# The value column that a transposing attention kernel multiplies apart: eight 32-column matmuls once in four steps, in place of four once in two

## The chip, the cores and the metric

The kernel runs on one core of one Trainium2 chip. The metric is device time in microseconds (us) of one execution. Five engines run their own instruction streams and meet at semaphores: TensorE (PE in the profile; PEld is its weight loads), VectorE (DVE), ScalarE (ACT), GpSimd (POOL) and SyncE (SP).

## The reference

Two layers, each cross-attention followed by a mixture of experts, on 1024 query rows of width 128 and a context of 6404 rows:

```python
x = x + tanh(g_xattn[0]) * L0_xattn(ctx, layernorm(x), mask, ...)   # keys: 6404 context rows and 1024 latents
x = x + tanh(g_ffn[0])   * L0_ffn(layernorm(x), ...)                # 8 experts, top 2
x = x + tanh(g_xattn[1]) * L1_xattn(layernorm(x), ctx, ...)         # keys: one null key and 6404 context rows
x = x + tanh(g_ffn[1])   * L1_ffn(layernorm(x), ...)
# both attentions: 16 heads of 64; softmax(q @ k.T) @ v, then an output projection
# L0 alone: q and k are each divided by the root mean square of their 64 elements (qn, kn)
```

The whole is float32. The kernel holds that precision by splitting operands into a high and a low part.

## The kernel before

The attention layer (`attention_layer`, called once with L = 0 and once with L = 1) works in 4 **groups** of 4 heads. Within a group, the keys are cut into tiles of 128; L0 has 59 tiles and L1 has 51. Four tiles are a **chunk**; L0 has 14 full chunks and L1 has 12, and 3 tiles are left as a tail. The loop is: group, chunk pair (a hardware loop), chunk of the pair (`half`), then `u` from 0 to 3, then the chunk's four tiles, taken two by two (`t` is 0, then 2). `u` picks a head pair (`u // 2`) and half of the queries (`u % 2`).

One **step** is one tile for one `u`: scores of 128 keys by 2 heads by 512 queries, an exponential, and the products with the values. One **unit** is the four steps of one `u`. There are 14 x 4 x 4 = 224 units in L0 and 12 x 4 x 4 = 192 in L1, beside a tail of 12 steps in each of the 8 groups. The two pairs of a unit are called the **first pair** (`t` is 0) and the **second pair** (`t` is 2) here.

TensorE's order in a pair is written out by hand:

1. `score` (L815), twice, for the two steps after this pair: 12 matmuls on 64 rows each (64*128 in the profile), two at a time beside each other, one on the upper and one on the lower half of the array. It waits until the exponentials of this pair's steps are done (`p_ready`).
2. `mix_last` (L823), twice: 4 matmuls with 32 weight columns (128*32). The output has 128 partitions: 64 high values of a head, 63 low values and the row of ones. The low part of the 64th value column has no room there; these matmuls compute it, in one bank (`spare_ps`, 32 partitions for each head and each parity of the step).
3. In the second pair only, `project_kv` (L796): 3 matmuls for keys and values of a tile of the next chunk. It writes the bank `proj_ps`, so it waits until VectorE has taken the low part of the keys out of that bank (`k_low`, L639).
4. `mix_high` (L833), twice: 4 matmuls of the probabilities' upper 16 bits, read as bfloat16, with the values. In the first pair each of the two halves of `out_ps` must have been added to `out_acc` by VectorE (`add_out`, L647).
5. `mix_low` (L840), twice: 4 matmuls of the probabilities' rest (`probs_lo`, made by VectorE in `p_lo`, L634).
6. In the first pair only, `transpose_k` (L802): two transposes of the projected key rows, which ScalarE then reads as `k_hi` (L547) and VectorE as `k_lo` (L639). In L0 GpSimd normalises these rows first (`k_norm`: a power, L485, then a product, L487), from a variance that VectorE computes (`k_var`, L619 and L621); in L1 it doesn't, and the transposes wait for ScalarE's copy alone.

VectorE's order in a unit is `p_lo` of the two steps of the second pair, `v_lo` (L627, L629), `k_low`, `p_lo` of the next unit's first two steps, `add_out` of the first half, `k_var`, `add_out` of the second half. ScalarE's is two exponentials (L553), then copies of keys or values. In the fourth unit of each chunk ScalarE also makes the high part of the next context chunk (L558) between two exponentials, and GpSimd its low part (`x_low`, L493).

A step's probabilities lie in buffer `n % NB` of `probs`. No engine waits for a buffer by name; the order of TensorE's work keeps a buffer from being written too early.

Of the kernel before, what the change touches and what calls it, by code (L numbers as in the profile page):

```python
# [40 lines left out]
GH = 4  # L41
NG = H // GH
CT = 4
NPAIR = GH // 2
NB = 4
NPL = 4
VW = 36
TAIL = 3
# [103 lines left out]
def attention_layer(nc, A, L, sem_, sb_, layer_norm, rstd, B):  # L152
# [7 lines left out]
    NFULL = (NTILES - TAIL) // CT  # L160
# [13 lines left out]
    with scope:  # L174
# [262 lines left out]
        def item_no(g, c, j):  # L437
            return g * NITEM + c * CT + j
# [4 lines left out]
        with nc.Block() as block:  # L443
# [343 lines left out]
            def _(pe):  # L787
# [31 lines left out]
                def mix_last(n_, u, t, par):  # L819
                    p, n = u // 2, u % 2  # L820
                    for e in range(2):
                        j = 32 * (2 * e + n_ % 2)
                        last = nc.tensor.matmul(last_ps[j:j + 32, :], vlast[:, par, 2 * p + e, t, 4 - 4 * n:36 - 4 * n],  # L823
                                                p_hi[:, n_ % NB, e * 512:(e + 1) * 512],
                                                start=False, stop=True, skip_group_check=True)
                    return last
# [30 lines left out]
                with pe.Fori(0, NG) as g:  # L857
                    def transpose_q(p):
                        for t in range(QT):
                            last = nc.tensor.transpose(scores[:, p, t * P:(t + 1) * P],  # L860
                                                       qf.rearrange("p (t a e) d -> p t a (e d)", a=NPAIR, e=2)[:, t, p, :],
                                                       ident[:, :])
                        last.then_inc(qt_done, 1)

                    pe.wait_ge(fin_read, ONE + g * QT)
                    project_kv(g, 0, 0)
                    transpose_k(g, 0, 0)
                    project_kv(g, 0, 1)
                    pe.wait_ge(q_final, g + 1)
                    transpose_q(0)  # L870
                    transpose_q(1)
                    transpose_k(g, 0, 1)
                    for j in range(2, CT):
                        project_kv(g, 0, j)
                        transpose_k(g, 0, j)
                    project_kv(g, 1, 0)
                    pe.wait_ge(q_lo_done, (g + 1) * NPAIR)
                    score(0, 0, 0, 0, item_no(g, 0, 0))
                    score(1, 0, 1, 0, item_no(g, 0, 1))
                    pe.wait_ge(e_read, ONE + g)  # L880
                    for j in range(4):
                        nc.tensor.matmul(last_ps[32 * j:32 * j + 32, :], zero32[:, :],
                                         vlast[:, 0, :, :, :].rearrange("p h t k -> p (h t k)")[:, 0:512],
                                         start=True, stop=True, skip_group_check=True)
                    with pe.Fori(0, PAIRS) as i:
                        for half in range(2):
                            c = i * 2 + half
                            for u in range(GH):
                                for t in range(0, CT, 2):
                                    n = (half * GH + u) * CT + t  # L890
                                    s = g * NSTEP + i * (2 * GH * CT) + n
                                    for k in range(2):
                                        n2 = n + 2 + k
                                        half2, u2, t2 = n2 // (GH * CT), n2 // CT % GH, n2 % CT
                                        item = g * NITEM + i * (2 * CT) + half2 * CT + t2 if u2 == 0 else None
                                        score(n2 % 2, u2, t2, half2 % 2, item, s + k)
                                    for k in range(2):
                                        if u == 0:
                                            pe.wait_ge(v_ready, item_no(g, c, t + k) + 1)
                                        pe.wait_ge(p_ready, s + k + 1)  # L900
                                        mix_last(n + k, u, t + k, half)
                                    if t == CT - 2:
                                        if u < GH - 1:
                                            project_kv(g, c + 1, u + 1)
                                        else:
                                            project_kv(g, c + 2, 0)
                                    for k in range(2):
                                        mix_high(n + k, u, t + k, half, g * NUNIT + c * GH + u)
                                    for k in range(2):
                                        mix_low(s + k, n + k, u, t + k, half, CT - 1)  # L910
                                    if t == 0:
                                        transpose_k(g, c + 1, u)
                    for n in range(0, GH * TAIL, 2):
                        s = g * NSTEP + NFULL * CT * GH + n
                        for k in range(2):
                            n2 = n + 2 + k
                            if n2 < GH * TAIL:
                                u2, t2 = n2 // TAIL, n2 % TAIL
                                if L == 1 and n2 == TAIL - 1:
                                    pe.wait_ge(null_fix, 3 + g + 1)  # L920
                                score(n2 % 2, u2, t2, 0, item_no(g, NFULL, t2) if u2 == 0 else None, s + k)
                        tiles = [(n + k, (n + k) // TAIL, (n + k) % TAIL) for k in range(2)]
                        for k, (n_, u, t) in enumerate(tiles):
                            if u == 0:
                                pe.wait_ge(v_ready, item_no(g, NFULL, t) + 1)
                            if L == 1 and n_ == TAIL - 1:
                                pe.wait_ge(null_in, (g + 1) * (16 * (2 + GH)))
                            pe.wait_ge(p_ready, s + k + 1)
                            last_e = mix_last(n_, u, t, 0)
                        same = tiles[0][1] == tiles[1][1]  # L930
                        for k, (n_, u, t) in enumerate(tiles):
                            mix_high(n_, u, t, 0, g * NUNIT + NFULL * GH + u)
                            if not same:
                                mix_low(s + k, n_, u, t, 0, TAIL - 1)
                        if same:
                            for k, (n_, u, t) in enumerate(tiles):
                                mix_low(s + k, n_, u, t, 0, TAIL - 1)
                    last_e.then_inc(e_done, 1)

                    project_q(g * (GH * DH) + GH * DH)  # L940

                    pe.wait_ge(o_added, (g + 1) * (2 * NUNIT) + 2 * ONE)
                    pe.wait_ge(e_read, ONE + g + 1)
                    pe.wait_ge(kn_ready if QK_NORM else kv_read, (g + 1) * NKV)
                    pe.wait_ge(we_in, (g + 1) * (16 * 4 * GH))
                    for t in range(QT):
                        if t >= 2:
                            pe.wait_ge(fin_read, ONE + g * QT + t - 1)
                        for h in range(GH):
                            at = (h // 2) * (D + 1)  # L950
                            e0 = DH * (h % 2)
                            nc.tensor.matmul(fin_bank(t, h % 2)[:, at:at + D + 1],
                                             oacc[:, h, t * P:(t + 1) * P],
                                             w_o[:, bass.ds(g * GH + h, 1), :].rearrange("p h n -> p (h n)"),
                                             start=h // 2 == 0, stop=False, skip_group_check=True)
                            last = nc.tensor.matmul(fin_bank(t, h % 2)[:, at:at + D],
                                                    esb[e0:e0 + DH, (t % 4) * P:(t % 4 + 1) * P], w_e[e0:e0 + DH, h, t // 4, :],
                                                    start=False, stop=True, skip_group_check=True)
                        last.then_inc(fin_mm, 1)
# [219 lines left out]
```

## Time and profile before

| | us |
|---|---|
| three runs | 4977.56, 4981.62 (median), 4983.63 |
| the profiled execution, its time | 4978.31 |
| its span, first to last instruction | 4976.5 |
| TensorE matmuls busy | 4373.9 (88%) |
| VectorE busy | 3684.0 (74%) |
| ScalarE busy | 2963.1 (60%) |
| GpSimd busy | 953.1 (19%) |

The span is the profiled execution from its first to its last instruction, and its own time is 1.8 us more. A matmul's end is modelled in the profile, so a matmul of 512 columns is listed with about 0.39 us while the next one starts about 0.23 us after it: lengths of stretches are taken from start to start. The main loops take 512 + 511 + 512 + 511 us in L0 and 428 + 427 + 428 + 428 us in L1, at a granted clock of 1.00 (2.4 GHz).

### The profile page before, as it was taken

What the parts mean: (1) busy time and instruction counts of PE and PEld (TensorE: products, weight loads), DVE (VectorE), ACT (ScalarE), POOL (GpSimd) and SP (SyncE); (2) the same over time, 40 slices, a digit from 0 to 9 for tenths busy, and PEclk for the clock granted to TensorE, in tenths of its full rate; (3) what the DMA queues carried; (4) which work ended last, traced back from release to release, by engine and by line L of the source; (5) the groups of instructions that cost most, each with busy time, mean ns of one, the idle gap of its engine ahead of it and who ended that gap; (6) DMA issues with size and microseconds to landing.
All of it is one profiled execution on the core that took longest, in us unless ns stands there. A gap on an engine that the chain in (4) does not pass through costs nothing. (4 is left out here: it accounts for less than half of the span.)

```text
span 4976.5 us, 75660 instructions
## 1 busy us (share of the span) xinstructions
PE 4373.9 (88%) x25271; PEld 2648.0 (53%) x25711; DVE 3684.0 (74%) x5350; ACT 2963.1 (60%) x4610; POOL 953.1 (19%) x687
## 2 busy tenths in 40 slices
PE   2899978999779998799989499979999799979996
PEld 1455544555545555455556355545555455545554
DVE  5788867888668886688861577757776677767775
ACT  2677736777457774677732377736774577647761
POOL 2333323333233332333310100000000000000000
PEclk7999988999889999899999699989999899989997
DMA  1000000000000000000000100000000000000000
GB/s 49 1 0 0 0 3 1 0 0 0 3 1 0 0 0 1 0 0 0 0 34 1 47 0 0 0 3 0 0 0 3 1 0 0 2 0 0 0 0 9
DMA packets 15438, 19.58 MB, mean 4 GB/s; under 512 B 2704, under 2 KB 11256, under 8 KB 15096
## 3 DMA queue, kind: packets, MB, share of 16 engines
q1 hardware_dynamic: 9204, 14.52, 1.0%
q10 hardware_dynamic: 6148, 3.89, 0.3%
q8 instruction: 57, 0.93, 0.1%
q14 instruction: 29, 0.24, 0.0%
HBM read 17.87 MB, written 0.52 MB: 4 GB/s over the span
## 5 line engine op out<-in xcount | busy, mean ns | idle before, releaser
L634 DVE TENSOR_TENSOR a_probs_lo<-a_probs 128x1024 fp32r<-128x1024 f32 x1760 | 2193.3, 1282 | 650.8 <-ACT a_probs L553 650.4
L553 ACT ACTIVATE a_probs<-scores_ps,a_c_neg 128x1024 f32<-128x1024 f32 x1760 | 1876.5, 1111 | 878.3 <-PE scores_ps L815 878.3
L840 PE MATMUL out_ps<-a_probs_lo,a_v 128*128 128x512 f32 x3520 | 1142.1, 445 | 0.0
L833 PE MATMUL out_ps<-a_probs,a_v 128*128 128x512 bf16 x3080 | 846.9, 388 | 87.9 <-issue 64.0
L815 PE MATMUL scores_ps<-a_q_hi,a_k_hi 64*128 64x512 f32 x3520 | 792.8, 445 | 6.7 <-DVE a_k_lo L751 5.9
L840 PEld LDWEIGHTS out_ps<-a_probs_lo,a_v 128*128 128x128 f32 x3520 | 660.9, 188 | 224.3
L815 PE MATMUL scores_ps<-a_q_lo,a_k_hi 64*128 64x512 f32 x3520 | 705.7, 393 | 0.0
L815 PE MATMUL scores_ps<-a_q_hi,a_k_lo 64*128 64x512 f32 x3520 | 700.7, 392 | 0.0
L647 DVE TENSOR_TENSOR a_out_acc<-out_ps,a_out_acc 128x512 f32<-128x512 f32 x896 | 598.5, 689 | 99.8 <-PE out_ps L840 91.3
L493 POOL TENSOR_TENSOR a_chunk_lo<-a_keys_in_T,a_chunk_hi 128x512 fp32r<-128x512 f32 x120 | 229.8, 1915 | 1792.4 <-ACT a_chunk_hi L558 1792.4
L485 POOL TENSOR_TENSOR a_k_stat<-a_k_stat,minus_half 128x4 f32<-128x4 f32 x244 | 247.6, 1015 | 1482.0 <-DVE a_k_stat L621 1482.0
L833 PEld LDWEIGHTS out_ps<-a_probs,a_v 128*128 128x128 f16 x3520 | 268.6, 96 | 471.3 <-issue 171.2
L815 PEld LDWEIGHTS scores_ps<-a_q_hi,a_k_hi 64*128 64x128 f32 x3520 | 333.5, 185 | 289.0 <-issue 251.9
L796 PE MATMUL proj_ps<-a_w_kv_hi,a_chunk_hi 128*128 128x512 f32 x456 | 238.2, 522 | 204.9 <-DVE a_k_lo L639 128.9
L547 ACT ACTIVATE a_k_hi<-proj_ps 128x256 fp32r<-128x256 f32 x448 | 172.5, 385 | 375.8 <-PE proj_ps L802 375.7
L487 POOL TENSOR_TENSOR normed<-normed,a_k_stat 128x256 f32<-128x256 f32 x244 | 373.4, 1530 | 19.1
L815 PEld LDWEIGHTS scores_ps<-a_q_lo,a_k_hi 64*128 64x128 f32 x3520 | 336.2, 185 | 74.5
L823 PE MATMUL spare_ps<-a_probs,a_v_last 128*32 128x512 bf16 x3520 | 360.2, 399 | 0.0
L526 ACT ACTIVATE normed<-proj_ps 128x256 f32<-128x256 f32 x456 | 174.0, 382 | 310.3 <-PE proj_ps L796 310.3
L815 PEld LDWEIGHTS scores_ps<-a_q_hi,a_k_lo 64*128 64x128 f32 x3520 | 336.2, 187 | 37.7
L543 ACT ACTIVATE a_v<-a_v 128x512 fp32r<-128x512 f16 x448 | 290.5, 648 | 0.1
L802 PE MATMUL proj_ps<-identity,normed 128*128 128x128 f32 x896 | 191.9, 297 | 99.5 <-POOL normed L487 89.0
(189 smaller groups left out, 3606.5 us busy)
## 6 DMA issues: line engine op xcount, KB each, us to landing
squares<-in_L_xattn_Wkv SPq DMA_DIRECT2D x16, 128.0 KB, 2.4
m_w<-in_L_ffn_w1T SPq DMA_DIRECT2D x1, 2048.0 KB, 7.7
m_w<-in_L_ffn_w2T SPq DMA_DIRECT2D x1, 2048.0 KB, 12.1
a_w_q<-in_L_xattn_Wq ACTq DMA_DIRECT2D x2, 512.0 KB
a_w_e<-in_L_xattn_Wout SPq DMA_DIRECT2D x64, 0.5 KB
a_w_e<-in_L_xattn_Wo SPq DMA_DIRECT2D x64, 0.5 KB
residual<-in_x SPq DMA_DIRECT2D x1, 512.0 KB, 3.9
a_w_o<-in_L_xattn_Wout ACTq DMA_DIRECT2D x1, 512.0 KB
```

What stands on the lines that cost most here:

```text
L485: nc.gpsimd.tensor_tensor(kst[:, 2, :], kst[:, 1, :], mhalf[:, 0:GH], ALU.pow).then_inc(kn_rstd, 1)
L487: nc.gpsimd.tensor_tensor(krow, krow, over(kst[:, 2, :], [P, GH, DH]), ALU.mult).then_inc(kn_ready, 1)
L493: nc.gpsimd.tensor_tensor(x_l[:, :], x, x_h[:, :].bitcast(F32), ALU.subtract).then_inc(x_lo, 1)
L543: nc.scalar.activation(v32[:, par, :, j, :], v16[:, par, :, j, :], ACT.Copy).then_inc(v_ready, 1)
L553: nc.scalar.activation(probs[:, n % NB, :], scores[:, n % 2, :], ACT.Exp, bias=cneg[:, p:p + 1]).then_inc(p_ready, 1)
L634: nc.vector.tensor_tensor(plow[:, n % NPL, :], probs[:, n % NB, :], p_hi[:, n % NB], ALU.subtract).then_inc(plo_ready, 1)
L647: nc.vector.tensor_tensor(oacc[:, 2 * p + e, q], outs[:, e * 512:(e + 1) * 512], oacc[:, 2 * p + e, q], ALU.add).then_inc(o_added, 1)
L796: last = nc.tensor.matmul(proj[:, :], x[:, j * P:(j + 1) * P], w[:, :], start=n == 0, stop=n == 2)
L815: last = nc.tensor.matmul(scores[:, b, e * 512:(e + 1) * 512], kk[r, par, p, t, :], qq[r, p, n * 512:(n + 1) * 512], start=m == 0, stop=m ...
L823: last = nc.tensor.matmul(last_ps[j:j + 32, :], vlast[:, par, 2 * p + e, t, 4 - 4 * n:36 - 4 * n], p_hi[:, n_ % NB, e * 512:(e + 1) * 512] ...
L833: nc.tensor.matmul(outs[:, e * 512:(e + 1) * 512], v16[:, par, 2 * p + e, t, :], p_hi[:, n_ % NB, e * 512:(e + 1) * 512], start=t == 0, st ...
L840: nc.tensor.matmul(outs[:, e * 512:(e + 1) * 512], v32[:, par, 2 * p + e, t, :], plow[:, n_ % NPL, e * 512:(e + 1) * 512], start=False, st ...
```

## The change

`mix_last` is no longer called for the two steps of each pair, but in the second pair for all four steps of the unit: none in the first pair, eight 128*32 matmuls in the second. In the tail it is called at the second, fourth and sixth of the six pairs, eight matmuls each. The probabilities of the first pair must be kept longer, so `probs` has eight buffers instead of four. The two waits for `p_ready` of a pair become one, for the later step, at the place of the first; those for `v_ready` too.

```diff
-NB = 4
+NB = 8
@@ the loop over u and t @@
-                                    for k in range(2):
-                                        if u == 0:
-                                            pe.wait_ge(v_ready, item_no(g, c, t + k) + 1)
-                                        pe.wait_ge(p_ready, s + k + 1)
-                                        mix_last(n + k, u, t + k, half)
+                                    if u == 0:
+                                        pe.wait_ge(v_ready, item_no(g, c, t + 1) + 1)
+                                    pe.wait_ge(p_ready, s + 2)
+                                    if t == CT - 2:
+                                        for k in range(CT):
+                                            mix_last(n + 2 - CT + k, u, k, half)
@@ the tail @@
-                        for k, (n_, u, t) in enumerate(tiles):
-                            if u == 0:
-                                pe.wait_ge(v_ready, item_no(g, NFULL, t) + 1)
-                            if L == 1 and n_ == TAIL - 1:
-                                pe.wait_ge(null_in, (g + 1) * (16 * (2 + GH)))
-                            pe.wait_ge(p_ready, s + k + 1)
-                            last_e = mix_last(n_, u, t, 0)
+                        seen = [t for _, u, t in tiles if u == 0]
+                        if seen:
+                            pe.wait_ge(v_ready, item_no(g, NFULL, seen[-1]) + 1)
+                        if L == 1 and TAIL - 1 in seen:
+                            pe.wait_ge(null_in, (g + 1) * (16 * (2 + GH)))
+                        pe.wait_ge(p_ready, s + 2)
+                        if n % 4 == 2:
+                            for m in range(n - 2, n + 2):
+                                last_e = mix_last(m, m // TAIL, m % TAIL, 0)
```

The order of instructions on TensorE, in the first pair of a unit of the main loop, before:

```order
 L815 MATMUL scores_ps<-a_q_lo,a_k_hi 128x512 x2
-L823 MATMUL spare_ps<-a_probs,a_v_last 32x512 x4
 L832 ISA
 L833 MATMUL out_ps<-a_probs,a_v 128x512
 L832 REGISTER_ALU
 L833 MATMUL out_ps<-a_probs,a_v 128x512 x3
 L840 MATMUL out_ps<-a_probs_lo,a_v 128x512 x4
 L800 REGISTER_ALU
 L802 MATMUL proj_ps<-identity,normed 128x128 x2
```

The row with the minus is gone, and `mix_high` stands right behind `score`. In the second pair of the same unit, on TensorE:

```order
 L815 MATMUL scores_ps<-a_q_lo,a_k_hi 128x512 x2
-L823 MATMUL spare_ps<-a_probs,a_v_last 32x512 x4
+L823 MATMUL spare_ps<-a_probs,a_v_last 32x512 x8
 L790 REGISTER_ALU
 L796 MATMUL proj_ps<-a_w_kv_hi,a_chunk_hi 128x512
 L796 MATMUL proj_ps<-a_w_kv_lo,a_chunk_hi 128x512
 L796 MATMUL proj_ps<-a_w_kv_hi,a_chunk_lo 128x512
 L833 MATMUL out_ps<-a_probs,a_v 128x512 x4
 L840 MATMUL out_ps<-a_probs_lo,a_v 128x512 x4
```

Here the same place, between `score` and `project_kv`, holds eight instead of four. On VectorE, ScalarE and GpSimd the order within the attention layers is the same as before.

## Rows read from the trace of the kernel before

**Rows 1.** The page: busy time of each engine, and the group of L823

```profile
PE 4373.9 (88%) x25271; PEld 2648.0 (53%) x25711; DVE 3684.0 (74%) x5350; ACT 2963.1 (60%) x4610; POOL 953.1 (19%) x687
...
L823 PE MATMUL spare_ps<-a_probs,a_v_last 128*32 128x512 bf16 x3520 | 360.2, 399 | 0.0
```

**Rows 2.** Timeline of an L0 unit, TensorE: start, length, instructions, [idle before]

```profile
1011.25 0.50 PE L815 MATMUL scores_ps<-a_q_hi,a_k_hi 64*128 64x512 f32 x2
...
1012.84 0.41 PE L823 MATMUL spare_ps<-a_probs,a_v_last 128*32 128x512 bf16 x4
...
1013.89 1.29 PE L840 MATMUL out_ps<-a_probs_lo,a_v 128*128 128x512 f32 x4
1015.15 0.44 PE L802 MATMUL proj_ps<-identity,normed 128*128 128x128 f32 x2
1015.52 0.51 PE L815 MATMUL scores_ps<-a_q_hi,a_k_hi 64*128 64x512 f32 x2
...
1017.10 0.41 PE L823 MATMUL spare_ps<-a_probs,a_v_last 128*32 128x512 bf16 x4
1017.44 0.50 PE L796 MATMUL proj_ps<-a_w_kv_hi,a_chunk_hi 128*128 128x512 f32 x1
1017.77 0.40 PE L796 MATMUL proj_ps<-a_w_kv_lo,a_chunk_hi 128*128 128x512 f32 x1
...
1018.24 1.07 PE L833 MATMUL out_ps<-a_probs,a_v 128*128 128x512 bf16 x4
...
1020.17 0.50 PE L815 MATMUL scores_ps<-a_q_hi,a_k_hi 64*128 64x512 f32 x2
```

**Rows 3.** Timeline of an L1 unit, TensorE

```profile
3494.44 1.29 PE L840 MATMUL out_ps<-a_probs_lo,a_v 128*128 128x512 f32 x4
3495.57 0.38 PE L802 MATMUL proj_ps<-identity,normed 128*128 128x128 f32 x2
```

**Rows 4.** Timeline of the first L0 unit of the first group, GpSimd and TensorE

```profile
152.26 0.69 POOL L487 TENSOR_TENSOR normed<-normed,a_k_stat 128x256 f32<-128x256 f32 x1
...
153.00 0.44 PE L802 MATMUL proj_ps<-identity,normed 128*128 128x128 f32 x2 [0.34 <-POOL normed L487]
153.37 0.49 PE L815 MATMUL scores_ps<-a_q_hi,a_k_hi 64*128 64x512 f32 x2
```

**Rows 5.** Timeline of the unit of rows 2, GpSimd

```profile
1012.42 1.01 POOL L485 TENSOR_TENSOR a_k_stat<-a_k_stat,minus_half 128x4 f32<-128x4 f32 x1 [6.26 <-DVE a_k_stat L621]
1013.51 1.58 POOL L487 TENSOR_TENSOR normed<-normed,a_k_stat 128x256 f32<-128x256 f32 x1
```

**Rows 6.** Timeline of the unit of rows 2, VectorE and ScalarE

```profile
1011.12 0.69 DVE L647 TENSOR_TENSOR a_out_acc<-out_ps,a_out_acc 128x512 f32<-128x512 f32 x1
...
1012.27 0.69 DVE L647 TENSOR_TENSOR a_out_acc<-out_ps,a_out_acc 128x512 f32<-128x512 f32 x1
...
1012.25 2.12 ACT L553 ACTIVATE a_probs<-scores_ps,a_c_neg 128x1024 f32<-128x1024 f32 x2 [1.11 <-PE scores_ps L815]
...
1013.40 1.22 DVE L634 TENSOR_TENSOR a_probs_lo<-a_probs 128x1024 fp32r<-128x1024 f32 x1 [0.44 <-ACT a_probs L553]
1014.54 1.63 DVE L634 TENSOR_TENSOR a_probs_lo<-a_probs 128x1024 fp32r<-128x1024 f32 x1
```

**Rows 7.** Waits over the whole span: who waited for whom, in total, times, longest

```profile
PEld proj_ps L802 <- POOL normed L487: 187.8, 236, 13.1
```

**Rows 8.** Timeline of an L0 fourth unit, which began at 1020.17

```profile
1026.55 0.41 DVE L639 TENSOR_TENSOR a_k_lo<-proj_ps,a_k_hi 128x256 fp32r<-128x256 f32 x1
1027.10 0.49 PE L796 MATMUL proj_ps<-a_w_kv_hi,a_chunk_hi 128*128 128x512 f32 x1 [0.64 <-DVE a_k_lo L639]
```

**Rows 9.** Timeline of a group's end, where TensorE changes between 128*128 and 64*128

```profile
695.40 0.49 PE L952 MATMUL out_ps<-a_w_o,a_out_acc 128*128 x2
695.82 0.48 PE L956 MATMUL out_ps<-a_w_e,squares 64*128 64x128 f32 x2
696.23 0.49 PE L952 MATMUL out_ps<-a_w_o,a_out_acc 128*128 x2
```

## The prediction

> **What bounds the kernel now.** The page comes first: TensorE is busy for 4373.9 us (88%), with 880 blocks of four `mix_last` matmuls (3520) [rows 1]. The share doesn't tell what ends a unit, so the timeline of one unit is read, from start to start. An L0 unit runs from 1011.25 to 1020.17, 8.92 us [rows 2]. Its first pair: scores 1.59 us (to 1012.84), then `mix_last`, `mix_high` and `mix_low`, transposes at 1015.15, the next scores at 1015.52. Its second pair: scores 1.58, `mix_last` 0.34 (1017.10 to 1017.44), projection 0.80 (to 1018.24), and 1.93 of `mix_high` and `mix_low`.
>
> Within a kind of block, 512-column matmuls start 0.23 to 0.24 apart (two such steps from 1017.77 to 1018.24), but a block's second one starts 0.33 after its first (1017.44, 1017.77) [rows 2]. Where the shape changes between 128*128, 64*128 and 128*32, TensorE loses about 0.1 us. The four 128*32 matmuls run beside each other: all four lie within 0.41 us, and the block behind starts 0.34 after them. So a `mix_last` block is one stream of about 0.23 plus 0.11 for one change of shape.
>
> So far TensorE looks like the bound in every unit. Two places say otherwise.
>
> The first is the transposes in L0. From the start of `mix_low` to the transposes it is 1.26 us in L0 (1013.89 to 1015.15) [rows 2] but 1.13 in L1 (3494.44 to 3495.57) [rows 3], for the same four matmuls. In L0 they wait for GpSimd's product, which ends at 13.51 + 1.58 = 1015.09 [rows 5], 0.06 before they start. The table of waits names this releaser 236 times, which is every key tile of L0 (4 groups x 59) [rows 7]. Read unit by unit, the transposes of all 224 L0 units begin 0.05 or 0.06 after that end. Now what releases GpSimd: VectorE adds out (1011.12) and computes the variance between its two `add_out` (1011.12 and 1012.27), GpSimd takes the power (1012.42) and begins the product at 1013.51, 0.11 after VectorE has begun `p_lo` (1013.40 to 1014.62). The product lasts 1.58 and ends 0.47 after `p_lo`; the second `p_lo` lasts 1.63 instead of 1.22, ending 1.08 after the product [rows 5, 6]. So the two take turns. All links count from the unit's start (1011.25): `add_out` begins 0.13 before it, the exponentials 1.00 after it (scores of the first step), `p_lo` at 2.15, the product's end at 3.84, the transposes at 3.90. None of them contains `mix_last`.
>
> The second place is the fourth unit of each chunk, 104 of the 416. There the projection waits for `k_lo`: it ends at 1026.96, the projection starts at 1027.10, 6.93 after the unit's start, with 0.64 idle [rows 8]. That chain too begins with the unit's scores, through exponentials and `p_lo`.
>
> **The change part by part.** Taken out of the first pair: 0.34 us of TensorE. Direct from scores (64*128) to `mix_high` (128*128) there is still one change of shape; the output stage does it both ways at like cost, 0.42 and 0.41 us for two matmuls and one change (695.40, 695.82, 696.23) [rows 9]. I take the removal as the whole 0.34.
>
> Added in the second pair: a second round of four. The trace has no 128*32 matmul that follows one on the same columns, so its cost is bounded from both sides. Below: if its weights load while the first round streams, it starts one stream later: 0.235 by half of the 0.47 in rows 2 (32-bit weights), and 512 columns at 2.4 GHz alone are 0.213. Above: if the weights can't load while the first round streams, it costs a full block, 0.34. I take 0.225, between the two lower figures, since both other shapes load weights under a running stream from the third matmul on. The block becomes 0.565.
>
> The page "TensorE: Matmul & The Clock Gate" of the Trainium skill (section "The mechanism") says that a weight load overlaps running matmuls only if its row group differs; both rounds use all 128 rows, so by it the second round is exposed, and the sum would be that of the rival "exposed" below. The trace doesn't agree for 128*128, where the same rows are loaded under a running stream; for 128*32 nothing here shows it.
>
> L1, normal units: 48 per group less 12 fourth ones, and less the group's first, which waits for other things: 4 x 35 = 140. Start to transposes, 0.13 less than in L0, thus 3.77 [rows 2, 3], becomes 3.43, nothing else is late there, and the second pair grows by 0.225: 0.115 less per unit, 140 x 0.115 = 16.1 us gained. The other cover to check is `out_ps`: `mix_high` now starts 1.59 after the unit's start instead of 1.93. The second `add_out` ends at about 12.27 + 0.69 = 1012.96 in L0, 1.71 after it, and goes with the second matmul of the block (1.83 after): just covered, and in L0 there is slack behind it anyhow. In L1 without the variance it ends about 0.55 earlier.
>
> L0, normal units: 4 x (56 - 14) = 168. TensorE could be at the transposes 0.34 + 0.12 = 0.46 earlier, but they still start 3.90 after the unit's start. The removal gains nothing; the wait takes its place. The second pair still grows by 0.225, and its end is the next unit's start. 168 x 0.225 = 37.8 us lost. The first unit of the first group shows such a long wait already: the transposes come after 0.34 of listed idle time, and the scores 0.37 behind them as in the others, so waiting adds no second cost [rows 4].
>
> Fourth units: the projection could start at 3.90 + 0.37 + 1.58 + 0.565 = 6.42 in L0 and still waits until 6.93. Nothing gained or lost, 104 x 0.
>
> Tails: six blocks of 0.34 become three of 0.565 per group, 2.04 - 1.70 = 0.34, eight groups: 2.8 us gained, as TensorE's stream is dense there.
>
> The merged waits cost nothing in the main loop: the scores ahead of them have already waited for both exponentials. Eight buffers cost no time, as nobody waits for a buffer.
>
> Sum: 37.8 - 16.1 - 2.8 = +18.9 us. Against the profiled execution, 4978.3 + 18.9 = 4997.2; the median of the runs is 3.3 above that execution, so **5000.5**, 0.38% slower.
>
> **Rivals.**
>
> *The gate opens* (faster). The order on the shared work of VectorE and GpSimd hangs on 0.11 us. If the product began ahead of `p_lo`, it would end near 2.26 + 0.69 = 2.95 after the unit's start (0.69 is its length in rows 4), long before TensorE needs it, and L0 would gain like L1: 168 x 0.115 = 19.3, all together 38.2 us, **4943**. It decides if `p_lo` slips by 0.11 against the variance. For it: the small margin. Against: both sides count from the same scores and from the same last `mix_low`, which the change leaves alone. "SBUF — State Buffer" of the Trainium skill (section "SBUF: two separate sides") calls the port pair of VectorE and GpSimd an exclusive lock, taken by whoever starts first; the turns in rows 5 and 6 agree, and by it the flip would be all or nothing.
>
> *Exposed.* The second round costs 0.34: 168 x 0.34 = 57 in L0, L1 and tails even: **5039**.
>
> *No change.* The gain of a change of shape is eaten in L0 just as much as it is won in L1, say if the second round costs 0.15 in L0 because its streams start before the first round's end (25 us lost, 27 gained in L1, with the tail 4 more): **4976 to 4985**. Nothing in the trace is shorter than 0.22 for 512 columns on the same array part.
>
> *The matmuls of the second round run one behind another*: 3 x 0.23 more per unit, 168 x 0.9 + 140 x 0.58: over 200 us. The first round's overlap speaks against it.
>
> That the change isn't made is excluded by the printed order.
>
> **How the numbers follow.** Forecast 0.62 (its own range 4990 to 5012, second round 0.21 to 0.26), exposed 0.13, gate opens 0.12, no change 0.10, one behind another 0.03. A measurement of this kernel tells 0.2% (10 us) from nothing. Faster: the gate, and a little of the second case, 0.14. Same: 0.12. Slower: 0.74. The range reaches from the upper part of "no change" over "exposed": 4984 to 5042; it leaves out the open gate and the serial case, under 2 in 10.
>
> **What would show it.** In L0, units of 9.15 us, transposes still 3.90 after the start and 0.05 behind GpSimd's product, `mix_low` to transposes 1.59. In L1, units of 8.64. Fourth units unchanged, 9.65 and 9.24. `mix_last` blocks of 0.56 to the next block. Wrong would be: blocks of 0.68, a product that starts ahead of `p_lo`, or transposes in L0 at 3.56.

## The result and the profile after

The changed kernel takes 5002.41 us (median of 6 runs, 5000.78 to 5004.48) where the kernel before takes 4980.66 (4977.56 to 4985.4). The ratio is 1.0044, with a 95% interval of 1.0033 to 1.0054: slower by 0.44%, 21.8 us. Forecast were 5000.5 us and 0.38%.

The page of the changed kernel, busy time and the group of L833 (`mix_high`), which now stands right behind the scores in every first pair:

```profile
span 4999.8 us, 75720 instructions
PE 4410.6 (88%) x25711; PEld 2622.4 (52%) x25711; DVE 3683.1 (74%) x5350; ACT 2997.4 (60%) x4610; POOL 953.9 (19%) x687
...
L833 PE MATMUL out_ps<-a_probs,a_v 128*128 128x512 bf16 x3520 | 952.0, 390 | 12.0 <-DVE a_out_acc L647 12.0
```

The shares tell nothing of a loss. The busy time of TensorE is 37 us more, but the page of before lists 25271 matmuls and this one 25711. The 440 that were missing are `mix_high` (3080 of 3520 listed before, all of them now): that is records, not work. As before, a unit has to be read from start to start. An L0 unit of the changed kernel, TensorE:

```profile
1014.55 0.51 PE L815 MATMUL scores_ps<-a_q_hi,a_k_hi 64*128 64x512 f32 x2
...
1016.15 1.08 PE L833 MATMUL out_ps<-a_probs,a_v 128*128 128x512 bf16 x4
1016.87 1.29 PE L840 MATMUL out_ps<-a_probs_lo,a_v 128*128 128x512 f32 x4
1018.47 0.44 PE L802 MATMUL proj_ps<-identity,normed 128*128 128x128 f32 x2 [0.31 <-POOL normed L487]
1018.83 0.51 PE L815 MATMUL scores_ps<-a_q_hi,a_k_hi 64*128 64x512 f32 x2
...
1020.41 0.64 PE L823 MATMUL spare_ps<-a_probs,a_v_last 128*32 128x512 bf16 x8
1020.98 0.50 PE L796 MATMUL proj_ps<-a_w_kv_hi,a_chunk_hi 128*128 128x512 f32 x1
...
1023.72 0.50 PE L815 MATMUL scores_ps<-a_q_hi,a_k_hi 64*128 64x512 f32 x2
```

Against [rows 2]: the scores are followed by `mix_high` at once, 1.60 after the unit's start. From `mix_low` to the transposes it is 1.60 where it was 1.26, and the transposes start 3.92 after the unit's start where it was 3.90. The eight matmuls take 0.57 to the next block (1020.41 to 1020.98) where four took 0.34. The unit is 9.17 long, before 8.92.

The same unit on GpSimd and VectorE, which answers to [rows 5, 6]:

```profile
1016.82 1.59 POOL L487 TENSOR_TENSOR normed<-normed,a_k_stat 128x256 f32<-128x256 f32 x1
```

```profile
1014.43 0.69 DVE L647 TENSOR_TENSOR a_out_acc<-out_ps,a_out_acc 128x512 f32<-128x512 f32 x1 [0.26 <-PE out_ps L840]
...
1016.71 2.78 DVE L634 TENSOR_TENSOR a_probs_lo<-a_probs 128x1024 fp32r<-128x1024 f32 x2 [0.45 <-ACT a_probs L553]
```

The product begins 2.27 after the unit's start, again 0.11 behind `p_lo` (1016.71), and ends at 1018.41, 0.06 ahead of the transposes. Nothing of this chain has moved. VectorE now waits 0.26 for TensorE before `add_out`.

The waits of the whole span, first of the kernel before, then of the changed one:

```profile
PE proj_ps L802 <- POOL normed L487: 89.0, 16, 12.4
PE proj_ps L796 <- DVE a_k_lo L639: 128.9, 128, 11.4
```

```profile
PE proj_ps L802 <- POOL normed L487: 157.1, 236, 12.3
PE proj_ps L796 <- DVE a_k_lo L639: 125.7, 128, 12.3
```

Listed idle time of TensorE ahead of the transposes grew by 68 us and now stands at every key tile of L0 (236 times): the removed matmuls, turned into waiting. The wait of the projection for `k_lo`, which the fourth units have, stayed (128.9 and 125.7).

An L1 unit of the changed kernel, TensorE:

```profile
3523.05 0.50 PE L815 MATMUL scores_ps<-a_q_hi,a_k_hi 64*128 64x512 f32 x2
...
3524.64 1.08 PE L833 MATMUL out_ps<-a_probs,a_v 128*128 128x512 bf16 x4
3525.36 1.29 PE L840 MATMUL out_ps<-a_probs_lo,a_v 128*128 128x512 f32 x4
3526.49 0.38 PE L802 MATMUL proj_ps<-identity,normed 128*128 128x128 f32 x2
...
3531.71 0.50 PE L815 MATMUL scores_ps<-a_q_hi,a_k_hi 64*128 64x512 f32 x2
```

Here nothing waits: 1.13 from `mix_low` to the transposes as in [rows 3], 3.44 from the unit's start, and the unit is 8.66 instead of 8.76.

### The profile page after: what moved, and what is told of

Same layout as the page of the kernel before. It is cut to its first block and busy times, and to the rows that moved or that the text cites. A ratio compares the mean times of both kernels' runs of the same rounds, so it can differ in the third digit from the quotient of the medians.

```text
span 4999.8 us, 75720 instructions
## 1 busy us (share of the span) xinstructions
PE 4410.6 (88%) x25711; PEld 2622.4 (52%) x25711; DVE 3683.1 (74%) x5350; ACT 2997.4 (60%) x4610; POOL 953.9 (19%) x687
## 5 line engine op out<-in xcount | busy, mean ns | idle before, releaser
L833 PE MATMUL out_ps<-a_probs,a_v 128*128 128x512 bf16 x3520 | 952.0, 390 | 12.0 <-DVE a_out_acc L647 12.0
L493 POOL TENSOR_TENSOR a_chunk_lo<-a_keys_in_T,a_chunk_hi 128x512 fp32r<-128x512 f32 x120 | 229.8, 1915 | 1775.8 <-ACT a_chunk_hi L558 1775.8
L833 PEld LDWEIGHTS out_ps<-a_probs,a_v 128*128 128x128 f16 x3520 | 280.2, 96 | 523.9 <-issue 218.6
L485 POOL TENSOR_TENSOR a_k_stat<-a_k_stat,minus_half 128x4 f32<-128x4 f32 x244 | 247.9, 1016 | 1519.0 <-DVE a_k_stat L621 1519.0
L796 PE MATMUL proj_ps<-a_w_kv_hi,a_chunk_hi 128*128 128x512 f32 x456 | 238.3, 522 | 200.3 <-DVE a_k_lo L639 125.7
L487 POOL TENSOR_TENSOR normed<-normed,a_k_stat 128x256 f32<-128x256 f32 x244 | 373.9, 1533 | 19.2
L796 PEld LDWEIGHTS proj_ps<-a_w_kv_hi,a_chunk_hi 128*128 128x128 f32 x456 | 88.4, 194 | 405.3 <-issue 189.5
```

What stands on the lines that cost most here:

```text
L485: nc.gpsimd.tensor_tensor(kst[:, 2, :], kst[:, 1, :], mhalf[:, 0:GH], ALU.pow).then_inc(kn_rstd, 1)
L487: nc.gpsimd.tensor_tensor(krow, krow, over(kst[:, 2, :], [P, GH, DH]), ALU.mult).then_inc(kn_ready, 1)
L493: nc.gpsimd.tensor_tensor(x_l[:, :], x, x_h[:, :].bitcast(F32), ALU.subtract).then_inc(x_lo, 1)
L796: last = nc.tensor.matmul(proj[:, :], x[:, j * P:(j + 1) * P], w[:, :], start=n == 0, stop=n == 2)
L833: nc.tensor.matmul(outs[:, e * 512:(e + 1) * 512], v16[:, par, 2 * p + e, t, :], p_hi[:, n_ % NB, e * 512:(e + 1) * 512], start=t == 0, st ...
```

## The experiments

Two theories were tested. A **gate** is here a place where TensorE must wait for another engine's work. The **gate theory**: in L0 the transposes wait for GpSimd's product, whose chain doesn't hold `mix_last`, so what is taken out of the first pair is lost as waiting, and what is added behind the transposes is paid in full. The **block theory**: TensorE bounds every normal unit alike, and a block of eight is dearer than two of four. Each run is compared with the kernel before on the same chip. In the table stand mean lengths of a unit in us, start to start, from each run's trace, without the units that begin a chunk pair. A normal unit is one of the first three of a chunk.

| run | median us | ratio (95% interval) | L0 normal | L0 fourth | L1 normal |
|---|---|---|---|---|---|
| before | 4980.66 | | 8.95 | 9.65 | 8.76 |
| changed | 5002.41 | 1.0044 (1.0033, 1.0054) | 9.17 | 9.65 | 8.66 |
| nb8_alone | 4978.18 | 0.9997 (0.9988, 1.0007) | 8.94 | 9.65 | 8.76 |
| new_in_L1_only | 4962.69 | 0.9966 (0.9954, 0.9978) | 8.95 | 9.65 | 8.67 |
| leave_first | 4928.93 | 0.9898 (0.9883, 0.9913) | 8.95 | 9.65 | 8.42 |
| leave_second | 4870.30 | 0.9780 (0.9765, 0.9795) | 8.60 | 9.65 | 8.43 |
| var_first_old | 4925.15 | 0.9889 (0.9874, 0.9904) | 8.77 | 9.22 | 8.76 |
| var_first_new | 4892.40 | 0.9824 (0.9811, 0.9837) | 8.65 | 9.23 | 8.66 |
| eight_in_first_pair | 4904.64 | 0.9850 (0.9837, 0.9864) | 8.65 | 9.65 | 8.65 |
| eight_first_var_first | 4883.95 | 0.9811 (0.9797, 0.9824) | 8.64 | 9.42 | 8.65 |
| split_early_old | 4933.82 | 0.9902 (0.9887, 0.9917) | 8.95 | 9.21 | 8.76 |
| split_early_new | 4956.30 | 0.9951 (0.9938, 0.9965) | 9.17 | 9.35 | 8.67 |
| split_early_eight_first | 4868.23 | 0.9774 (0.9760, 0.9787) | 8.64 | 9.38 | 8.65 |
| all_three | 4893.13 | 0.9822 (0.9809, 0.9836) | 8.64 | 9.91 | 8.65 |

### One part alone: the buffers

```diff
-NB = 4
+NB = 8
```

> The old order with eight probability buffers instead of four, nothing else. Both theories: no engine waits for a buffer, so 4981 us within 0.1%, L0 units of 8.93 and L1 units of 8.76 us. A rival for the whole change, that the larger tile itself costs (other addresses), expects up to the 22 us that the change lost, about 5002.

4978.18, no difference that can be told. The larger tile costs nothing that can be measured.

### One part alone: the change without L0's main loop

```diff
+if L == 0:
+    for k in range(2):
+        mix_last(n + k, u, t + k, half)
-if t == CT - 2:
+elif t == CT - 2:
```

> The change's kernel, but with the old four-in-each-pair order in L0's main loop (tails and L1 as changed). Gate theory (in L0 the transposes wait for GpSimd, so the removal gains nothing there and the second round is pure loss; in L1 nothing waits): L0 loops back to 511.5 us, L1 loops 424.3, tails 0.37 less: 4981 - 15.6 - 3.0 = 4962. Rival (a block of eight costs more than two of four wherever it stands, by 22 us over 416 units): L1 carries 192/416 of the loss, 4991.

4962.69. The change is a gain in L1 and the tails; all of the loss is in L0.

### Half of the matmuls left out

These two take the changed kernel and issue four `mix_last` only in one of the two pairs.

```diff
 if t == CT - 2:          # leave_second: if t == 0
-    for k in range(CT):
-        mix_last(n + 2 - CT + k, u, k, half)
+    for k in range(2):
+        mix_last(n + k, u, t + k, half)
```

> Leaves out part of the computation: the four mix_last matmuls of every first pair in the main loop aren't issued, those of the second pair are. Gate theory: L0 units stay at 8.93 (0.34 of TensorE's work taken out for nothing, all of it becomes wait before the transposes), L1 normal units lose 0.34: 140 x 0.34 = 48, tails 3: 4930. Rival (TensorE bounds all normal units): 308 x 0.34 = 105 + 3 less, 4873.

> Leaves out part of the computation: the four mix_last matmuls of every second pair in the main loop aren't issued, those of the first pair are. Gate theory: behind the transposes TensorE is the bound in both layers, so every normal unit loses 0.34, L0 8.59 and L1 8.42, fourth units (9.65, 9.24) nothing: 308 x 0.34 = 105, tails 3: 4873. The rival expects the same here; the difference to the run without the first pair's is what tells them apart (57 us by the gate theory, 0 by the rival).

4928.93 and 4870.30: the same four matmuls are worth 59 us more when they are taken out of the second pair than out of the first. A TensorE stretch of an L0 unit without those of the first pair:

```profile
920.23 0.51 PE L815 MATMUL scores_ps<-a_q_hi,a_k_hi 64*128 64x512 f32 x2
...
921.83 1.08 PE L833 MATMUL out_ps<-a_probs,a_v 128*128 128x512 bf16 x4
922.54 1.29 PE L840 MATMUL out_ps<-a_probs_lo,a_v 128*128 128x512 f32 x4
924.14 0.44 PE L802 MATMUL proj_ps<-identity,normed 128*128 128x128 f32 x2 [0.30 <-POOL normed L487]
```

The transposes start 3.91 after the unit's start, as with the matmuls. The block theory, which expected 4873 for both, falls.

### The gate moved: the variance first

VectorE's `k_var` stands ahead of both `add_out`; once with the old order of `mix_last` (var_first_old), once with the change (var_first_new).

```diff
 p_lo(s0 + 5, 1)
+k_var(...)
 add_out(s0 + CT - 1, u, 0)
-k_var(...)
 add_out(s0 + CT - 1, u, 1)
```

> The old order of mix_last, but VectorE computes the variance of the key rows ahead of both add_out instead of between them, about 0.7 us earlier. In L1 nothing changes. Gate theory: GpSimd's product then starts about 1.6 us after the unit's start, ahead of p_lo (2.15), and is done before the transposes: L0 normal units fall from 8.93 to L1's 8.76 (168 x 0.17 = 29 us). In L0's fourth units x_low starts earlier too, as in L1, and they fall from 9.65 to about 9.24 (56 x 0.42 = 23 us). Together 4929. Rival (the wait before the transposes is something else of L0, GpSimd only happens to end there): 4981.

> The change, and the variance ahead of both add_out. Gate theory: with the gate out of the way the change gains in L0 what it gains in L1, 0.115 us in each normal unit: L0 normal units 8.64, fourth units 9.24, L1 as in the change: 4890, so 39 us under the same edit on the old order, where the change alone was 22 us above the old order. Rival (the block of eight is dear by itself in L0): again about 20 us above it, 4950.

4925.15 and 4892.40. Without the gate the change gains 33 us (39 expected) where it lost 22 with it: the same edit of `mix_last`, the other sign. GpSimd and then VectorE in an L0 unit of var_first_new, which begins at 941.82:

```profile
942.05 1.01 POOL L485 TENSOR_TENSOR a_k_stat<-a_k_stat,minus_half 128x4 f32<-128x4 f32 x1 [7.16 <-DVE a_k_stat L621]
943.14 0.61 POOL L487 TENSOR_TENSOR normed<-normed,a_k_stat 128x256 f32<-128x256 f32 x1
```

```profile
943.97 2.36 DVE L634 TENSOR_TENSOR a_probs_lo<-a_probs 128x1024 fp32r<-128x1024 f32 x2 [0.78 <-ACT a_probs L553]
```

The product starts ahead of `p_lo` and lasts 0.61 instead of 1.58; the two `p_lo` last 2.36 instead of 2.78. So both had been held up by each other, 1 us on GpSimd and 0.4 on VectorE. That agrees with the exclusive lock of the Trainium skill's "SBUF — State Buffer" (section "SBUF: two separate sides"), though not to the last tenth: the late product ends 0.47 behind the first `p_lo`, a little less than its own 0.61. Only the times are shown; what the two engines share isn't.

### The block of eight in the other pair

In the first pair, for the last two steps of the unit before and the pair's own.

```diff
-if t == CT - 2:
-    for k in range(CT):
-        mix_last(n + 2 - CT + k, u, k, half)
+if t == 0 and n > 0:
+    for k in range(2):
+        mix_last(n - 2 + k, (u - 1) % GH, CT - 2 + k, half if u else 1 - half)
+if t == 0 or n == 2 * GH * CT - 2:
+    for k in range(2):
+        mix_last(n + k, u, t + k, half)
```

> Eight mix_last once in four steps, but in the first pair: the two steps of the unit before and the pair's own two (at the first unit of a chunk pair four, and four at the end of its last). The variance is where it was. Gate theory: in L0 the block of 0.565 lies in the slack before the transposes; TensorE gets to them 4.00 after the unit's start, 0.1 behind the gate, and the second pair loses 0.34: L0 normal units 8.64 (168 x 0.29 = 49 us), L1 116 x 0.115 + 24 x 0.34 = 21.5, tails 3, fourth units nothing: 4907. Rival (it doesn't matter in which pair the block stands): 5002 as in the change.

4904.64. TensorE of an L0 unit:

```profile
947.24 0.50 PE L815 MATMUL scores_ps<-a_q_hi,a_k_hi 64*128 64x512 f32 x2
...
948.83 0.63 PE L823 MATMUL spare_ps<-a_probs,a_v_last 128*32 128x512 bf16 x8
...
951.25 0.38 PE L802 MATMUL proj_ps<-identity,normed 128*128 128x128 f32 x2
```

GpSimd and then VectorE in the same unit:

```profile
949.69 1.40 POOL L487 TENSOR_TENSOR normed<-normed,a_k_stat 128x256 f32<-128x256 f32 x1
```

```profile
949.39 2.78 DVE L634 TENSOR_TENSOR a_probs_lo<-a_probs 128x1024 fp32r<-128x1024 f32 x2 [0.26 <-ACT a_probs L553]
```

The transposes start 4.01 after the unit's start without a wait: the block of eight lies where the slack was. The same eight matmuls, once in four steps, cost 98 us less than in the change. The product begins 0.30 behind `p_lo` here instead of 0.11 and lasts 1.40 instead of 1.59, so that it ends 3.85 after the unit's start as before. In all 140 normal L0 units of either kernel it ends 0.47 behind the first `p_lo`, whenever it began: its end follows `p_lo`, not its own start.

> Eight in the first pair, and the variance ahead of both add_out. Gate theory: the gate lay 0.1 ahead of TensorE already, so L0's regular normal units stay at 8.64; the 28 units with a block of four lose 0.16 (4.5 us), and L0's fourth units 0.42 (23 us) because x_low starts earlier: 4879. If L0's fourth units stay at 9.65, their chain isn't what I think: 4902.

4883.95, and the normal L0 units stay at 8.64 as the theory has it. But the fourth units are 9.42 instead of 9.22 or so. Their GpSimd and VectorE, in a unit that begins at 922.90:

```profile
924.79 0.61 POOL L487 TENSOR_TENSOR normed<-normed,a_k_stat 128x256 f32<-128x256 f32 x1
925.74 1.89 POOL L493 TENSOR_TENSOR a_chunk_lo<-a_keys_in_T,a_chunk_hi 128x512 fp32r<-128x512 f32 x1 [0.34 <-ACT a_chunk_hi L558]
```

```profile
925.07 3.65 DVE L634 TENSOR_TENSOR a_probs_lo<-a_probs 128x1024 fp32r<-128x1024 f32 x2 [0.22 <-ACT a_probs L553]
```

With the shorter second pair, the last `p_lo` and the variance behind it come later against the unit's start. The product begins 1.89 after it (1.33 in var_first_new), still first, but now runs into `p_lo`, and each seems to push the next: product, `p_lo`, `x_low` (1.89 instead of 1.69), `p_lo`, 0.2 later at the end. No run takes this chain apart.

### The fourth units: the context chunk split early

ScalarE's `x_high` moves from the fourth unit's exponentials to the end of the third, and GpSimd's `x_low` ahead of its last `k_norm` of the chunk; with the old order, with the change, with the eight in the first pair, and with that and the variance first (all_three).

```diff
-if t == 0 and k == 1 and u == GH - 1:
-    x_high(c + 2)
 ...
 v_wide(g, c + 1, u, 1 - half)
+if u == GH - 2:
+    x_high(c + 2)
 ...
-for j in range(1, CT):
+for j in range(1, CT - 1):
     k_norm(g, c + 1, j)
 x_low(g, c + 3, c + 2)
+k_norm(g, c + 1, CT - 1)
```

> The old order of mix_last; ScalarE makes the high part of the next context chunk at the end of the third unit instead of between the fourth unit's two exponentials, and GpSimd makes the low part ahead of its last key normalisation of the chunk. My theory of the fourth units (their chain of exponentials, p_lo and k_lo is late by this work alone): they become units like the others, L0 9.65 to 8.95, L1 9.22 to 8.76: 56 x 0.70 + 48 x 0.46 = 61 us, 4919. Rival (the projection in the fourth unit is late for another reason): 4980.

> The change with the same edit. Fourth units are no longer shielded by their own chain, so they take the change as the others do: in L0 9.17, 0.225 above the old order; in L1 8.66, 0.1 under it. 22 + 56 x 0.225 - 48 x 0.1 = 30 us above the old order with this edit: 4949. If the fourth units took no part in the change for another reason, 22 us above: 4941.

4933.82 and 4956.30, where 4919 and 4949 were expected. In L1 the projection's wait was due to this work: all but the last fourth unit of a loop became 8.75. In L0 they fell to 9.21 only, 0.44 of the 0.70 expected. The difference by the change, 22.5 us, is that of the kernels without this edit, not the 30 expected; by the time alone the shielding isn't shown. The trace has fourth units taking part, 9.21 to 9.35 in L0 and 0.10 less in L1, but less than normal ones, since in L0 the moved `x_low` makes their own transposes late (4.19 after the unit's start with the old order, 4.10 with the change, against 3.91 in normal units).

> Eight in the first pair (variance where it was), and the context chunk split early. All units as the normal ones of the run with eight in the first pair, 8.65 in both layers: 4904.6 - 56 x 1.0 - 48 x 0.57 = 4821. Rival: GpSimd's low part, now between normalisations, delays the last one and the transposes with it, fourth L0 units 9.0 or more: 4840.

> Eight in the first pair, variance ahead of both add_out, context chunk split early. L0's and L1's units 8.64, the units with a block of four 8.40: 4884 - 56 x 0.78 - 48 x 0.57 = 4813. It shows whether the variance's place still matters once the block of eight covers the wait: 5 to 8 us by the 28 units with a block of four, not more.

4868.23 and 4893.13, both misses (4821 and 4813), and the rival named for the first is what happened, at a higher price (4840): its fourth L0 units have their transposes 4.53 after the start, where its normal ones have them at 4.01. GpSimd, VectorE and TensorE in a fourth L0 unit of all_three, which begins at 931.79 (this kernel's lines lie one higher, except L485, L487 and L493):

```profile
932.73 1.30 POOL L493 TENSOR_TENSOR a_chunk_lo<-a_keys_in_T,a_chunk_hi 128x512 fp32r<-128x512 f32 x1 [7.09 <-ACT a_chunk_hi L559]
933.98 2.06 POOL L485 TENSOR_TENSOR a_k_stat<-a_k_stat,minus_half 128x4 f32<-128x4 f32 x1
936.12 0.66 POOL L487 TENSOR_TENSOR normed<-normed,a_k_stat 128x256 f32<-128x256 f32 x1
```

```profile
933.95 2.36 DVE L635 TENSOR_TENSOR a_probs_lo<-a_probs 128x1024 fp32r<-128x1024 f32 x2 [0.22 <-ACT a_probs L554]
```

```profile
936.84 0.44 PE L803 MATMUL proj_ps<-identity,normed 128*128 128x128 f32 x2 [0.88 <-POOL normed L487]
```

`x_low` holds GpSimd until 934.03; the power of four elements comes behind it, a moment after `p_lo` began, and takes 2.06 instead of 1.01. The transposes start 5.05 after the unit's start. 56 units of 9.91 instead of 8.64 are 71 of the 80 us missed. split_early_eight_first is the fastest kernel measured, 2.3% under the kernel before, with its fourth L0 units at 9.38 still the longest. GpSimd's old order in L0 and the new one in L1 wasn't tried.

## Why the prediction was right

**The size of the sum.** L0's normal units grew from 8.95 to 9.17, 0.228 each (0.225 forecast); with the units that begin a chunk pair the four loops grew by 37.7 us (37.8). L1's loops shrank by 15.1 (16.1), the tails by 0.37 each, 3.0 (2.8). Together +19.6 by the traces, +18.9 forecast, and +21.8 by the medians. The two profiled executions are 23.3 apart; 3.2 of what the loops and tails leave lies behind L1's last tail, where split_early_old, without the change, has 3.3 more than the kernel before and eight_in_first_pair, with eight at once, 0.1: it isn't the change's. The time itself came out 1.9 from the forecast and the difference 2.9; the one point between them is chance, since the forecast started from the median of three runs, 4981.62, and six gave 4980.66.

**The second round.** It was put between 0.213 and 0.34 and taken at 0.225: 0.34 became 0.57, so it costs 0.23. The weight loads of the block of 1020.41 show why:

```profile
1020.41 0.12 PEld L823 LDWEIGHTS spare_ps<-a_probs,a_v_last 128*32 128x32 f16 x8 [0.36 <-issue]
```

All eight are done within 0.12 us, those of the second round while the first streams, on the same rows. The rule of the Trainium skill's "TensorE: Matmul & The Clock Gate" (section "The mechanism"), that row groups must differ, doesn't hold here, and the rival "exposed" falls with it. The same section also lets a load to the background weight buffer run ahead; the trace names no buffer, but its loads run ahead as that sentence has it, and the prediction had left it out.

**The gate.** That the removal gains nothing in L0 is shown by three independent edits: left out (leave_first), gate moved (var_first), slack filled (eight_in_first_pair). The rival "the gate opens" didn't come about by itself, as the margin of 0.11 stayed; var_first_new shows that it would have had the sign and mechanism named. Its price was set too low: 4943, where var_first_new took 4892. The rival gave a normal L0 unit the 0.115 of L1, but with the gate goes the wait that was there before the change, so these units fell by 0.30 (8.95 to 8.65), which makes about 29 us more for all 168. The gate had cost such a unit 0.18 and not 0.12, as var_first_old shows (8.95 to 8.77): 0.13 ahead of the transposes, and 0.06 behind them, where the scores start 0.31 after transposes that didn't wait and 0.37 after those that did. A further 24 us come from the fourth units, 9.65 to 9.23, since `x_low` comes earlier.

**The fourth units** kept 9.65 in L0, as forecast. The split_early runs show that in L1 the split of the context chunk alone made them late. In L0 it was part of it: moving it took 0.44 away and made their transposes late instead, so what they would be without it isn't shown.

**No cost of the merged waits or the buffers:** nb8_alone for the buffers, and new_in_L1_only for both, whose L0 loops take 2046.0 us together as before (2045.9).

## What to carry to other kernels

Before moving work within a unit, find what each stretch between two gates waits for: work taken from ahead of a gate that another engine's chain opens is worth nothing, and put behind it is paid in full. The same block of eight made the kernel 22 us slower behind the gate and 76 us faster ahead of it. A gate that shows almost no idle time (0.13 us here, found by comparing one stretch between two layers) is a gate all the same, and taking it away was worth 0.18 us a unit even without the change.

## What the runs showed of the hardware

- A second round of four 128*32 matmuls on the same columns costs 0.23 us for 512 columns, 0.57 for the block of eight against 0.34 for four.
- GpSimd's product of 128x256 took 0.61 ahead of VectorE's 128x1024 subtraction, 1.58 to 1.59 when it began 0.11 behind it and 1.40 when it began 0.30 behind it; in both it ended 0.47 behind the subtraction. A power of 128x4 elements took 1.01, and 2.06 when it began 0.03 behind such a subtraction.
- What these two engines cost each other depends on where their work falls: with eight `mix_last` moved from the second pair to the first, fourth L0 units came out 0.2 longer (9.23 and 9.42), and with `x_low` 1.9 us earlier, ahead of the power and the product, 0.5 longer still (9.42 and 9.91).
